# Products with the values of eight heads in one piece: a fused two-layer kernel with attention on one Trainium2 core

## What is computed

```python
x = x + tanh(g_xattn[0]) * L0_xattn(layernorm(x), ctx, mask)
x = x + tanh(g_ffn[0])   * L0_ffn(layernorm(x))
x = x + tanh(g_xattn[1]) * L1_xattn(layernorm(x), ctx)
x = x + tanh(g_ffn[1])   * L1_moe(layernorm(x))

# attention, 16 heads of 16
q, k, v = (split into heads: x @ Wq.T, ctx @ Wk.T, ctx @ Wv.T)
attn = softmax(q @ k.T / 4)        # layer 0: masked
out = (attn @ v) @ Wo.T + bo
```

## Time and profile before

| what | value |
| --- | --- |
| median of 3 runs | 1286.76 us (1285.56 to 1288.77) |
| profiled execution, first to last instruction (its span) | 1284.1 us |
| PE busy | 1213.3 us, 94% |
| DVE busy | 893.2 us, 70% |
| ACT busy | 710.7 us, 55% |
| POOL busy | 481.3 us, 37% |
| first attention stage | about 45 to 460 us |
| feed-forward | about 479 to 765 us |
| second attention stage | about 764 to 1130 us |
| experts | up to the end |

### The profile page before, as it was taken

One profiled execution on the slowest core, in us unless ns is written; L12 is line 12 of the kernel. 1 busy time (PEld: TensorE's weight loads), 2 busy tenths in 40 slices (PEclk: granted clock), 3 DMA queues, 4 the chain that ended last, 5 costly groups with the idle time before them and its releaser, 6 DMA issues.

```text
span 1284.1 us, 25175 instructions
## 1 busy us (share of the span) xinstructions
PE 1213.3 (94%) x9260; PEld 859.1 (67%) x9260; DVE 893.2 (70%) x2680; ACT 710.7 (55%) x1197; POOL 481.3 (37%) x675
## 2 busy tenths in 40 slices
PE   7899999999999989999999989999999999988998
PEld 6577666666767654444458866677676776578987
DVE  4677677876787646589999856767867868652333
ACT  2455555555655538889973426666566566622221
POOL 5534333443443100067000334344643643322555
PEclk9899999999999999999999999999999999998999
DMA  6423333233432041000004653355455342137973
GB/s 194 127 77 105 91 93 108 88 105 98 123 88 67 11 128 55 1 1 2 1 1 130 177 157 108 108 152 147 129 167 136 113 134 72 51 145 241 311 194 39
DMA packets 121942, 137.22 MB, mean 107 GB/s; under 512 B 12882, under 2 KB 116428, under 8 KB 121798
## 3 DMA queue, kind: packets, MB, share of 16 engines
q1 hardware_dynamic: 111888, 125.98, 33.2%
q0 software_dynamic: 7296, 8.15, 3.5%
q10 hardware_dynamic: 2634, 1.49, 0.5%
HBM read 58.42 MB, written 27.36 MB: 67 GB/s over the span
## 4 chain that ended last, share of the span: by engine, by line
PE 55%; DVE 6%; issue 3%; ACT 2%; POOL 1%; SPq 1%; DMA 1%; ACTq 0%; POOLq 0%; DVEq 0%
PE PS L669 14%; PE PS L715 6%; PE PS L470 5%; PE PS L410 5%; PE PS L683 4%; PE PS L453 4%; PE PS L429 4%; PE PS L528 2%; PE PS L724 2%; PE PS L502 2%; PE PS L417 2%; DVE NM L1119 1%; PE PS L546 1%; ACT P L839 1%; PE PS L511 1%
## 5 line engine op out<-in xcount | busy, mean ns | idle before, releaser
L839 ACT ACTIVATE P<-PS 128x512 f32<-128x512 f32 x512 | 302.4, 601 | 165.8 <-PE PS L456 100.2
L1116 DVE CUSTOM_DVE_ANT_0 MX<-PS,NQ 128x256 bf16<-128x256 f32 x512 | 192.5, 418 | 73.3 <-PE PS L429 73.0
L453 PE MATMUL PS<-QS,KS 99*128 99x256 bf16 x1024 | 226.6, 275 | 7.7 <-ACT P L839 6.7
L1119 DVE TENSOR_REDUCE NM<-PS 128x2 f32<-128x512 f32 x256 | 173.5, 685 | 74.6 <-PE PS L429 72.9
L429 PE MATMUL PS<-KS,QS 96*128 96x256 bf16 x1024 | 196.9, 275 | 21.6 <-DVE NM L1116 13.4
L429 PEld LDWEIGHTS PS<-KS,QS 96*128 96x128 bf16 x1024 | 87.2, 98 | 86.6 <-DVE NM L1116 26.1
L470 PE MATMUL PS<-P,V 128*32 128x256 f32 x2048 | 137.7, 387 | 1.5 <-ACT P L839 1.5
L453 PEld LDWEIGHTS PS<-QS,KS 99*128 99x128 bf16 x1024 | 95.4, 99 | 53.3 <-ACT P L839 20.1
L456 PE MATMUL PS<-NK,identb 128*128 128x256 bf16 x512 | 128.2, 275 | 0.0
L669 PE MATMUL PS<-XNT,wup 128*128 128x512 f16 x576 | 124.9, 379 | 0.0
L669 PEld LDWEIGHTS PS<-XNT,wup 128*128 128x128 f16 x576 | 56.2, 98 | 67.3
(11 more groups left out here) (233 smaller groups left out, 2473.6 us busy)
## 6 DMA issues: line engine op xcount, KB each, us to landing
KS<-PP SPq DMA_DIRECT2D x192, 128.0 KB, 2.9
QS<-PP SPq DMA_DIRECT2D x192, 128.0 KB, 2.5
WH<-in_wex SPq DMA_DIRECT2D x16, 768.0 KB, 8.0
WG<-in_wex SPq DMA_DIRECT2D x10, 768.0 KB, 5.1
bufd<-bias_row SPq DMA_DIRECT2D x5, 1032.0 KB, 12.0
XB<-in_x SPq DMA_DIRECT2D x16, 256.0 KB, 2.8
CT<-in_ctxT SPq DMA_DIRECT2D x16, 256.0 KB, 3.1
x1d<-XB SPq DMA_DIRECT2D x16, 256.0 KB, 2.1
```

The costliest lines, as they stand in the source:

```text
L453: ins = tensor.matmul(o, t.KS[b % 3][0:99, h, 128 * kt:128 * kt + 128], t.QS[b % 3][0:99, h, :], start=True, stop=(L == 1))
L839: scalar.activation(t.P[h % 8][:, :, :], PS[:, h % 2, :].rearrange("p (k n) -> p k n", k=2), ACT.Exp).then_inc(s_ex, 1)
L1116: ins = vector.tensor_tensor_reduce(t.MX[:, 2 * (h % 2) + qt, :], PS[:, bk, 256 * qt:256 * qt + 256], t.NQ[b % 4][:, qt, :], -1.0, 1.0e30, ...
L1119: ins = vector.tensor_reduce(nm[:, :, h], PS[:, bk, :].rearrange("p (t n) -> p t n", t=2), X, ALU.max, negate=True)
```

## The change

Products of eight heads are issued as one piece: `pe_av` takes hh = 0 or 1 instead of g = 0 to 3. It is called in slot 9 for heads 0 to 7 and in slot 1 of the next step for heads 8 to 15. Slots 5 and 13 lose their pieces. The number of products is the same. There are ten probability buffers, used in turn over all heads, instead of eight, and one OT instead of two. The copies to OT move on ACT from slot 12 to slot 10 and from slot 3 to slot 2. The thresholds of `s_ah` follow the new count, two a block.

```diff
+NP_RING = 10
...
-            t.P = [tile(m, f"P{i}", [128, 2, 256], F32) for i in range(8)]
-            t.OT = [tile(m, f"OT{i}", [128, 4, 256], F32) for i in range(2)]
+            t.P = [tile(m, f"P{i}", [128, 2, 256], F32) for i in range(NP_RING)]
+            t.OT = tile(m, "OT", [128, 4, 256], F32)
...
-        def pe_av(L, b, g):
+        def pe_av(L, b, hh):
...
             pe.wait_ge(s_v, n + 1)
-            pe.wait_ge(s_ex, 16 * n + 4 * g + 4)
-            if g % 2 == 0:
-                pe.wait_ge(s_ot, 2 * (n - 1) + g // 2 + 1)
-            for kt in range(2):
-                for i in range(4):
-                    h = 4 * g + i
-                    ins = tensor.matmul(PS[32 * i:32 * i + 32, ob, 256 * (g % 2):256 * (g % 2) + 256],
-                                        t.V[b % 3][:, kt, h, :], t.P[h % 8][:, kt, :], start=(kt == 0), stop=(kt == 1))
+            pe.wait_ge(s_ex, 16 * n + 8 * hh + 8)
+            pe.wait_ge(s_ot, 2 * (n - 1) + hh + 1)
+            for g in range(2):
+                for kt in range(2):
+                    for i in range(4):
+                        h = 8 * hh + 4 * g + i
+                        ins = tensor.matmul(PS[32 * i:32 * i + 32, 4 + hh, 256 * g:256 * g + 256], t.V[b % 3][:, kt, h, :],
+                                            t.P[(16 * n + h) % NP_RING][:, kt, :], start=(kt == 0), stop=(kt == 1))
             ins.then_inc(s_ah, 1)
...
-                if k in (5, 9, 13):
-                    pe_av(L, s, (k - 5) // 4)
+                if k == 9:
+                    pe_av(L, s, 0)
...
                 if k == 1:
-                    pe_av(L, s - 1, 3)
+                    pe_av(L, s - 1, 1)
...
-            act.wait_ge(s_ah, 4 * n + h // 4 - 1)
+            act.wait_ge(s_ah, (i - NP_RING) // 8 + 1)
...
-            act.wait_ge(s_otr, 2 * (n - 1))
-            act.wait_ge(s_ah, 4 * n + 2 * hh + 2)
+            act.wait_ge(s_otr, 2 * n)
+            act.wait_ge(s_ah, 2 * n + hh + 1)
...
-            act.wait_ge(s_ah, 4 * (n - 2))
+            act.wait_ge(s_ah, 2 * (n - 2))
...
-            if 0 <= s < NB and k == 12:
+            if 0 <= s < NB and k == 10:
                 act_heads(L, s, 0)
...
-                if k == 3:
+                if k == 2:
                     act_heads(L, s - 1, 1)
...
-                sp.wait_ge(s_ah, 8 * NB)
+                sp.wait_ge(s_ah, 4 * NB)
```

More of the change, by code:

```diff
@@ L457, in pe_scores_t @@
             ins.then_inc(s_st, 1)
-        def pe_av(L, b, g):
+        def pe_av(L, b, hh):
             n, t = L * NB + b, TL[L]
-            ob = 4 + g // 2
             pe.wait_ge(s_v, n + 1)
-            pe.wait_ge(s_ex, 16 * n + 4 * g + 4)
-            if g % 2 == 0:
-                pe.wait_ge(s_ot, 2 * (n - 1) + g // 2 + 1)
-            for kt in range(2):
-                for i in range(4):
-                    h = 4 * g + i
-                    ins = tensor.matmul(PS[32 * i:32 * i + 32, ob, 256 * (g % 2):256 * (g % 2) + 256],
-                                        t.V[b % 3][:, kt, h, :], t.P[h % 8][:, kt, :], start=(kt == 0), stop=(kt == 1))
+            pe.wait_ge(s_ex, 16 * n + 8 * hh + 8)
[6 more added lines that the diff above has]
+                                            t.P[(16 * n + h) % NP_RING][:, kt, :], start=(kt == 0), stop=(kt == 1))
             ins.then_inc(s_ah, 1)
@@ L510, in pe_heads @@
             for g in range(4):
-                ins = tensor.transpose(PS[:, bk, 128 * g:128 * g + 128], t.OT[b % 2][:, g, 128 * qt:128 * qt + 128],
+                ins = tensor.transpose(PS[:, bk, 128 * g:128 * g + 128], t.OT[:, g, 128 * qt:128 * qt + 128],
                                        ident[:, :])
@@ L836, in act_exp @@
             i = 16 * n + h
-            act.wait_ge(s_ah, 4 * n + h // 4 - 1)
+            act.wait_ge(s_ah, (i - NP_RING) // 8 + 1)
             act.wait_ge(s_st, i + 1)
-            scalar.activation(t.P[h % 8][:, :, :], PS[:, h % 2, :].rearrange("p (k n) -> p k n", k=2),
+            scalar.activation(t.P[i % NP_RING][:, :, :], PS[:, h % 2, :].rearrange("p (k n) -> p k n", k=2),
                               ACT.Exp).then_inc(s_ex, 1)
@@ L843, in act_heads @@
             n, t = L * NB + b, TL[L]
-            act.wait_ge(s_otr, 2 * (n - 1))
-            act.wait_ge(s_ah, 4 * n + 2 * hh + 2)
-            scalar.activation(t.OT[b % 2][:, 2 * hh:2 * hh + 2, :], PS[:, 4 + hh, :].rearrange("p (g n) -> p g n", g=2),
+            act.wait_ge(s_otr, 2 * n)
+            act.wait_ge(s_ah, 2 * n + hh + 1)
+            scalar.activation(t.OT[:, 2 * hh:2 * hh + 2, :], PS[:, 4 + hh, :].rearrange("p (g n) -> p g n", g=2),
                               ACT.Copy).then_inc(s_ot, 1)
```

## The result

The changed kernel took 1300.26 us (median of 4 runs, 1297.66 to 1302.18), the kernel before 1286.85 beside it: a ratio of 1.0103, with a 95% interval of 1.0087 to 1.012. It is slower by 13.4 us, where +9.2 was forecast. The profiled execution took 1297.66 us for a span of 1296.4.

The account below looks back on a forecast made before the run. PE was taken to set the pace (busy 1213.3 of 1284.1 us). Second layer +7.7 and first layer +1.5 summed to +9.2 us on 1286.8, giving 1296.0 us, range 1285 to 1303.

Parts of the forecast that it names:

- The 2.7 us from span to median: Whole time: the kernel before had a median of 1286.76 us, 2.7 above its profiled span; this difference was carried over.
- What a piece costs: On PE: four heads take 1.09 us, eight heads 0.86 more; each merge saves 0.23, 14.7 us in all.
- Second layer, slot 13: Without its piece PE saves 0.41 us, not 1.09, as s(13) waits for DVE's maxima; with slot 1, +0.45 a block.
- Slots 5 to 8: Second layer: 0.72 us saved of 1.09, limited by POOL's remainder and DVE's ON; with slot 9, +0.14 a block.
- The ten steady blocks: Second layer, 10 of 16 blocks: each 0.45 + 0.14 us longer, +5.9 us in all.
- Routing blocks: Three second-layer blocks where s(12) already waits for DVE: 0.86 - 0.67 us each, +0.6 us in all.
- Ends of the second layer: First and last blocks of that layer: about +1.2 us, from the longer last piece and slots paced by exponentials.
- First layer: Eight blocks give -2.2 us, seven whose s(0) is at or near a DVE wait +2.8, ends +0.9: +1.5 us.
- Ring, OT and ACT's order costed at nothing: Ten buffers, single OT and earlier ACT copies cost nothing; QF's 0.44 us idle absorbs most of a 0.48 delay.
- All comes through: Rival: the full 14.7 us of saved PE work shows, 1272.1 us, with no new DVE waits; chance 0.14.
- The first layer gains: Rival: slot 5's 1.09 us carries through DVE to slot 13, -9.3 us over 16 blocks, about 1287; chance 0.16.
- ACT's order costs more: Rival: the OT copy delays QF, POOL and L1125, 0.3 to 0.5 us in 26 blocks, 1300 to 1305; chance 0.15.

## Why the prediction was right, point by point

- **The direction and its reason** held: PE loses work, and DVE's chains give less back than slots 1 and 9 take. PE's busy time fell by 9.0 us, where "some 14" was forecast. A part of the missing 5 can be the way busy time is counted: the first 0.16 us of a wait behind a short matmul still count as busy (see the bullet on the first layer). That was not added up.
- **The time** came out at +13.4 us for +9.2, inside the range. In the traces it is +12.3: 4.9 us more than the sum in the second layer, 1.7 less in the first. The 2.7 us from span to median that I carried over hold more than the overhead of an execution: in the profiled one of the changed kernel time and span lie 1.3 us apart. How near the sum came is in part luck, since errors cancel: the clock took 1.7 us in one layer and gave 1.5 in the other.
- **What a piece costs** held: +0.86 for eight heads, and 0.23 for a merge that nothing hides (22.80 against 23.03).
- **Second layer, slot 13** held: 0.41 forecast, 0.40 measured, hence +0.465 a block for +0.45.
- **Slots 5 to 8** held as a sum, 0.66 saved for 0.72, but the place was wrong. I looked for the wait at the transposes of ON in slot 8. It is at the router in slot 7, which needs the bank that ON of slot 5 frees. Steady blocks are 0.66 longer for 0.59.
- **The ten steady blocks** cost 7.7 us where 5.9 was forecast: 0.7 of it from those 0.07, the rest from s(0), which waits for DVE in blocks 7 and 11 (0.24 each), and from blocks 1 and 6 (0.44 and 0.30 more; block 10 takes 0.14 less). I had taken all ten as equal.
- **Routing blocks**: 0.20, 0.20 and 0.27 for the 0.2 forecast each, but for slot 13 of block 9, where +1.69 came from the clock (below). No term of the sum had the clock in it.
- **Ends of the second layer**: 2.5 us where 1.2 stood, an estimate without rows. Some 1.1 of it is there in the kernel with the ring and the copies alone (0.58 and 0.49), so it is ACT's order, which I had costed at nothing.
- **First layer**: -0.2 where +1.5 stood, and the difference is the clock. In block 3 the profiled execution of the kernel before had a stretch at half the granted clock in slots 8 and 9, and so have all other kept traces but that of the changed kernel. View by windows of before, and then of the changed kernel, granted clock third from the end:

```profile
134.80:138.20 3.40, 3.08 (x21) 1.90 (x24) 3.40 (x14) 1.20 (x2) 0.83 (x4) 0.50 0.00 0
134.40:137.80 3.40, 3.40 (x46) 2.16 (x47) 3.37 (x17) 1.08 (x2) 0.84 (x4) 1.00 0.12 33
```

  The two slots are 0.41 and 0.14 shorter in the changed kernel. In the kernel with the change in the first layer alone, which has the stretch, they are unchanged and 0.97 longer: 1.5 us between the two. There the layer takes 0.63 more from its first st to its last, and with the 0.86 of the last piece behind it that is the +1.5 forecast.

  The sum was right, but by luck in its parts. Slots 8 of blocks 1 and 12 took 1.03 and 0.73 more, which no term had, and the wait in slot 10 was mis-sized the other way. I took the 0.28 in the bracket for the whole of it. The kernel before at that place, ahead of the row at 356.43:

```profile
355.88 0.27 PE L456 MATMUL PS<-NK,identb 128*128 128x256 bf16 x1
```

  The timeline of the changed kernel has no wait there:

```profile
352.29 0.27 PE L457 MATMUL PS<-NK,identb 128*128 128x256 bf16 x1
352.40 0.38 PE L430 MATMUL PS<-KS,QS 96*128 96x256 bf16 x2
```

  The spacing is 0.11. Before it was 0.55, and 0.44 of that was wait. The bracket counts from the modelled end of the matmul ahead (0.27 long, 0.11 to the next start) and leaves out 0.16 of every such wait. Slot 10 gave 0.45 to 0.51 in nine blocks, 4.2 us in the whole layer, where 3.1 (0.28 in 11 blocks) was put.
- **Ring, OT and ACT's order costed at nothing** held for a steady block. At the ends ACT's order cost 1.8 us, which the sum lacks. In the steady blocks of the second layer the reason was not the whole one. The cover was not QF's idle time alone: with the copies where they were, the transposes would have been late by 0.55, hidden by the wait for ON.
- **The rivals.** "All comes through" failed at slot 13, as weighed. "The first layer gains" was half right: each steady block gains with the merge of heads 0 to 7 alone (0.69), and the merge of heads 8 to 15 takes it back at slots 13 and 0. "ACT's order costs more" gave a time close to the measured one (1300 to 1305) by a mechanism that did not occur in a steady block: its chain runs through QF, and POOL's remainder started 3.54 us behind st(3) (1062.76 to 1066.30) as before, 3.55 (1029.28 to 1032.83). Its own arithmetic was off, too: 0.3 to 0.5 us in 26 blocks is 8 to 13 us, and not 8 at most.

## What to carry to other kernels

Before a piece of work is taken out of a slot, ask of the products behind it on the same engine for how long it covered their inputs. Here a merge of two pieces is worth 0.23 us where nothing is late (heads 0 to 7 of the second layer, with DVE's order changed) and costs 0.47 where DVE's chain comes 0.7 us too late (heads 8 to 15). Test the two halves of a merge apart: one half and one swap on DVE made a kernel 0.6% faster than before out of a change that was 1.0% slower. Measure a wait of PE as the spacing of starts less the unhindered spacing, not by the idle time in the brackets. And before two profiled executions are compared term by term, look for stretches at half the clock that only one of them has.

## What the runs showed of the hardware

Behind PE's idle time in slots 12 and 13 the granted clock fell in some blocks. Timeline of the changed kernel in block 9 of the second layer:

```profile
1001.98 0.39 PE L430 MATMUL PS<-KS,QS 96*128 96x256 bf16 x2 [0.87 <-DVE NM L1119]
...
1003.56 0.39 PE L430 MATMUL PS<-KS,QS 96*128 96x256 bf16 x2 [0.97 <-DVE NM L1119]
1003.79 3.43 PE L502 MATMUL PS<-XNT 128*128 128x256 f32 x8
```

And the windows around it:

```profile
1000.00:1003.80 3.80, 1.96 (x16) 1.17 (x15) 3.73 (x10) 2.15 (x4) 0.82 (x1) 1.00 0.01 3
1003.80:1007.00 3.20, 3.20 (x10) 2.33 (x9) 2.64 (x12) 0.00 (x0) 1.15 (x2) 0.53 0.01 3
```

PE worked for 1.96 of 3.80 us, and then the clock was granted at half, 1.2 instead of 2.4 GHz, just when work was there: the projection of the values took 3.43 us instead of 1.89. It isn't certain to come. With the middle part behind ON the same place has the same two waits and the full clock:

```profile
1005.89 0.39 PE L430 MATMUL PS<-KS,QS 96*128 96x256 bf16 x2 [0.92 <-DVE NM L1119]
...
1007.47 0.39 PE L430 MATMUL PS<-KS,QS 96*128 96x256 bf16 x2 [0.97 <-DVE NM L1119]
1007.70 1.89 PE L502 MATMUL PS<-XNT 128*128 128x256 f32 x8
```

And the window of that kernel:

```profile
1006.30:1009.50 3.20, 2.23 (x13) 1.73 (x12) 3.17 (x11) 0.60 (x1) 1.60 (x2) 1.00 0.02 5
```

What decides between the two cases was not tried. Where the clock falls, the place costs more than the wait itself, here up to 1.7 us. The kernels that empty slot 13 of the second layer showed such a fall in one or two of blocks 1 to 13, the kernels that keep its piece in none; that the idle time causes it was not shown by a run that changes nothing else. The stretch in block 3 of the first layer, in 13 of the 14 kept traces, is just as little certain: ahead of it PE waits 1.77 us for s(8) in the kernel before and in the changed one alike, and only the former has it.
